# A graph layer on one core: 17 instead of 16 superblocks looked up by a one-hot product, predicated copies in PSUM, and another layout of the turned rows

## What is computed

```python
def reference(x, src, dst, edge_attr_64, edge_weight1, W_node, W_review):
    h = jnp.maximum(_layernorm(x, axis=-1), 0.0)      # 12500 x 16
    m = (h @ W_node.T)[src] + edge_attr_64 @ W_review.T   # 400000 edges
    m = m * edge_weight1
    return x + jax.ops.segment_sum(m, dst, num_segments=12500)
```

## Time and profile before

| what | value |
|---|---|
| median of 3 runs | 1766.9 us (1765.85 to 1771.57) |
| profiled execution, its own time | 1771.62 us |
| its span | 1769.5 us |
| mean granted TensorE clock | 0.942 of full |
| TensorE matmul busy | 1544.8 us (87%), 25,040 instructions |
| VectorE busy | 1455.6 us (82%), 3,393 |
| GpSimd busy | 1247.3 us (70%), 1,177 |
| ScalarE busy | 970.8 us (55%), 4,245 |
| DMA | 195.34 MB, mean 110 GB/s |
| chain that ended last | PE 46%, DVE 24%, issue 12%, DVEq 8%, POOL 6% |

### The profile page before, as it was taken

The page is one execution under the profiler, slowest core; times in us unless marked ns, Lnnn a source line. Parts: engine busy times, 40 slices in busy tenths (PEclk is TensorE's granted clock), DMA queues, the critical chain, the costliest instruction groups (busy, mean ns, idle before and its releaser), DMA issues.

```text
span 1769.5 us, 75737 instructions
## 1 busy us (share of the span) xinstructions
PE 1544.8 (87%) x25040; PEld 1524.7 (86%) x25040; DVE 1455.6 (82%) x3393; ACT 970.8 (55%) x4245; POOL 1247.3 (70%) x1177
## 2 busy tenths in 40 slices
PE   0119998999989899999989998998989998999977
PEld 0019998999989899999989898998989898999975
DVE  7998887888888787888888787878878887878864
ACT  1114364665656564756656564756656564756653
POOL 2287777777777777777777777777777777777400
PEclk9659999999999999999999999999999999999965
DMA  3524345454545445454444454454545454554443
GB/s 116 92 36 113 100 114 114 110 122 103 125 106 128 112 114 127 104 129 109 118 113 111 116 120 116 118 125 105 118 110 114 115 125 109 122 130 100 119 86 48
DMA packets 513913, 195.34 MB, mean 110 GB/s; under 512 B 475071, under 2 KB 496196, under 8 KB 513212
## 3 DMA queue, kind: packets, MB, share of 16 engines
q1 hardware_dynamic: 474853, 178.88, 39.9%
q0 software_dynamic: 36000, 9.29, 5.9%
q10 hardware_dynamic: 2609, 1.55, 0.5%
HBM read 186.67 MB, written 2.92 MB: 107 GB/s over the span
## 4 chain that ended last, share of the span: by engine, by line
PE 46%; DVE 24%; issue 12%; DVEq 8%; POOL 6%; ACT 2%; DMA 1%; ACTq 0%; POOLq 0%; SPq 0%
PE found L1110 26%; PE seg L1143 11%; POOL vals_p L530 6%; DVE big L770 5%; PE seg L1134 5%; DVEq L875 4%; PE edge_h L1124 3%; DVE masked L824 3%; DVEq L867 2%; DVE perm L860 2%; DVE masked L838 1%; DVE mid L845 1%; ACT mid L592 1%; DVE by_rank L715 1%; DVE by_rank L714 1%
## 5 line engine op out<-in xcount | busy, mean ns | idle before, releaser
L530 POOL DMA_INDIRECT vals_p<-h_ext,idx_t x1125 | 1228.7, 1092 | 350.9 <-issue 330.6
L1110 PE MATMUL found<-table,big 128*128 128x112 f16 (+2 forms) x16384 | 870.6, 215 | 57.8 <-DVE by_rank L888 32.3
L1110 PEld LDWEIGHTS found<-table,big 128*128 128x128 f16 x16384 | 846.1, 100 | 63.9 <-DVE by_rank L888 34.9
L592 ACT ACTIVATE sel_p<-hit_p,wgt_t 128x64 f32<-128x64 f16 x1125 | 292.8, 335 | 429.2 <-DVE hit_p L845 416.2
L592 ACT ACTIVATE mid<-mid,wgt_t 128x64 f32<-128x64 f16 x2000 | 500.1, 333 | 36.8 <-DVE mid L845 34.9
L1143 PE MATMUL seg<-mid 128*96 128x64 f32 x4000 | 400.4, 256 | 15.9 <-ACT mid L612 11.3
L1143 PEld LDWEIGHTS seg<-mid 128*96 128x96 f32 x4000 | 379.3, 173 | 18.0 <-ACT mid L592 11.8
L770 DVE TENSOR_SCALAR big<-low_all,own 128x2004 f16<-128x2004 f16 x516 | 361.2, 742 | 2.8 <-DMA low_all<-low_dram 2.8
L879 DVE SCALAR_TENSOR_TENSOR acc<-seg,count_s,acc 96x64 f32 x400 | 112.2, 280 | 168.5 <-issue 126.8
L1134 PE MATMUL seg<-sel_p,vals_p 128*80 128x64 f32 x2250 | 201.8, 237 | 6.9 <-DMA vals_p<-h_ext,idx_t 6.9
L1134 PEld LDWEIGHTS seg<-sel_p,vals_p 128*80 128x80 f32 x2250 | 183.3, 154 | 7.8 <-DMA vals_p<-h_ext,idx_t 3.8
(11 more groups left out here) (131 smaller groups left out, 546.1 us busy)
## 6 DMA issues: line engine op xcount, KB each, us to landing
low_all<-low_dram SPq DMA_DIRECT2D x128, 501.0 KB
mid<-in_edge_attr_dram SPq DMA_DIRECT2D x400, 160.0 KB
vals_p<-in_edge_attr_dram SPq DMA_DIRECT2D x232, 160.0 KB
vals_p<-h_ext,idx_t POOLq DMA_INDIRECT x1125
big<-in_dst_dram SPq DMA_DIRECT2D x1, 1562.5 KB
big<-in_edge_weight_dram SPq DMA_DIRECT2D x1, 1562.5 KB
h_ext<-mid SPq DMA_DIRECT2D x2, 781.2 KB
low_all<-low_dram ACTq DMA_DIRECT2D x2, 501.0 KB
```

The costliest lines, as they stand in the source:

```text
L530: pool.indirect_dma_start(vals_p[:, q % RP, j, R:F], None, h_ext, bass.IndirectOffsetOnAxis(ap=idx_t[:, q * J + j:q * J + j + 1], axis=0), ...
L592: last = nc.scalar.activation(sel[:, j, :], hit[:, j, :], ACT.Copy, scale=wgt_t[:, bass.ds(tile + j, 1)])
L1110: last = nc.tensor.matmul(found[x % 2][:, r * P:r * P + n], hot[:, x // 2 % 2, a, col:col + P], rows, start=(a == 0 and part == 0), stop=( ...
```

## The change

One superblock moves from the gathered edges to the sorted ones: 8 and 17 in place of 9 and 16. That is 200 gathered groups (1,000 indirect DMAs in place of 1,125) and 425 sorted ones, and the loop runs over 16 phases in place of 15. A loop phase has 12 gathered groups, at steps 4 to 15, in place of 14; the first phase has 8, at steps 8 to 15, in place of 15. There are 6 slots for them in place of 7.

The choice among the candidates is made inside `found`, without masks for each candidate: `mark` takes the three bits of the digit and a `valid` flag; where bit 2 is set candidates 4 and up are copied over 0 and up, where bit 1 is set 2 and 3 over 0 and 1, where bit 0 is set 1 over 0; the row that is left is multiplied by `valid` into `found_h`. `masked` is gone, and TensorE waits for `chosen` of the step two before. The four operations are spread over VectorE's step in another way than the four before.

`by_rank` is ordered list, half, feature, so that the 32 values of a list lie next to each other; the casts and the split read PSUM and write `by_rank` in this order.

```diff
-GATHERED = 9
-SORTED = 16
+GATHERED = 8
+SORTED = 17
-RP = 7
-FIRST = 2
+RP = 6
+FIRST = 4
+FIRST0 = 8
 PER_STEPS = STEPS - FIRST
+PER_FIRST = STEPS - FIRST0
...
-        by_rank = by_rank_raw[:, 0:LISTS * H].bitcast(F16).rearrange("p (i f l) -> p i f l", i=2, f=H)
+        by_rank = by_rank_raw[:, 0:LISTS * H].bitcast(F16).rearrange("p (l i f) -> p l i f", i=2, f=H)
...
         def turned_ranks(i):
-            return turn_bank[i].rearrange("p (f l) -> p f l", l=P)[:, :, 0:C]
+            return turn_bank[i].rearrange("p (f l) -> p l f", l=P)[:, 0:C, :]
...
-                        nc.scalar.copy(by_rank[:, 0, i * PART_F:(i + 1) * PART_F, :], turned_ranks(i)).then_inc(rank_top, 1)
+                        nc.scalar.copy(by_rank[:, :, 0, i * PART_F:(i + 1) * PART_F], turned_ranks(i)).then_inc(rank_top, 1)
...
                 def mark(u):
-                    nc.vector.tensor_tensor(mask[:], digit_now[:, bass.ds(u, 1), :].rearrange("p o j -> p (o j)").unsqueeze(1).to_broadcast([C, WIDEST, P]),
-                                            digit[0:C, :].unsqueeze(2).to_broadcast([C, WIDEST, P]), ALU.is_equal).then_inc(mask_in, 1)
+                    nc.vector.tensor_tensor(bits[:], digit_now[:, bass.ds(u, 1), :].rearrange("p o j -> p (o j)").unsqueeze(1).to_broadcast([C, BITS, P]),
+                                            bit_no[:].unsqueeze(2).to_broadcast([C, BITS, P]), ALU.bitwise_and).then_inc(bits_in, 1)
+                    nc.vector.tensor_tensor(valid[:], digit_now[:, bass.ds(u, 1), :].rearrange("p o j -> p (o j)"), limit[:], ALU.is_lt).then_inc(bits_in, 1)
...
-                    nc.vector.tensor_tensor(masked[:], rows_of(x, 0, FOLD), masks_of(x, 0, FOLD), ALU.mult).then_inc(masked_low, 1)
-                    nc.vector.copy_predicated(masked[:, :, 0:WIDTH[x] - FOLD, :], masks_of(x, FOLD, WIDTH[x]), rows_of(x, FOLD, WIDTH[x])).then_inc(masked_in, 1)
-                    nc.vector.tensor_tensor(masked[:, :, 0:2, :], masked[:, :, 0:2, :], masked[:, :, 2:4, :], ALU.add).then_inc(folded, 1)
-                    nc.vector.tensor_tensor(found_h[:, x * RANKS:(x + 1) * RANKS, :], masked[:, :, 0, :], masked[:, :, 1, :], ALU.add).then_inc(chosen, 1)
+                    if WIDTH[x] > HALF:
+                        nc.vector.copy_predicated(rows_of(x, 0, WIDTH[x] - HALF), bit_of(x, 2, WIDTH[x] - HALF), rows_of(x, HALF, WIDTH[x])).then_inc(upper_in, 1)
+                    nc.vector.copy_predicated(rows_of(x, 0, 2), bit_of(x, 1, 2), rows_of(x, 2, 4)).then_inc(pair_in, 1)
+                    nc.vector.copy_predicated(rows_of(x, 0, 1), bit_of(x, 0, 1), rows_of(x, 1, 2)).then_inc(one_in, 1)
+                    nc.vector.tensor_tensor(found_h[:, x * RANKS:(x + 1) * RANKS, :], rows_of(x, 0, 1).rearrange("p j b f -> p j (b f)"),
+                                            valid[:, x * RANKS:(x + 1) * RANKS].unsqueeze(2).to_broadcast([C, RANKS, H]), ALU.mult).then_inc(chosen, 1)
...
                     for step in range(STEPS):
                         if step:
-                            mask_low(u, step - 1)
-                            copy_high(u, step - 1)
+                            copy_upper(u, step - 1)
                         make_hot(u, step)
                         if step:
-                            fold_four(u, step - 1)
+                            copy_pair(u, step - 1)
                         if step:
                             add_of_p(step - 1)
-                            fold_two(u, step - 1)
+                            copy_one(u, step - 1)
                         if step + 1 < STEPS:
                             for g in groups_unsorted(step + 1):
                                 make_perm(t, g)
                         if step:
+                            keep_valid(u, step - 1)
                             add_of_s(step - 1, 0)
...
                     if x >= 2:
-                        if WIDTH[x - 2] == FOLD:
-                            pe.wait_ge(masked_low, ps * (SORTED * STEPS) + u * STEPS + (x - 1))
-                        else:
-                            pe.wait_ge(masked_in, ps * (SORTED * COPIES[STEPS]) + u * COPIES[STEPS] + COPIES[x - 1])
+                        pe.wait_ge(chosen, ps * (SORTED * STEPS) + u * STEPS + (x - 1))
...
-                                                by_rank[:, :, :, g * J + q].rearrange("p i f -> p (i f)"), start=True, stop=True)
+                                                by_rank[:, g * J + q].rearrange("p i f -> p (i f)"), start=True, stop=True)
```

More of the change, by code:

```diff
@@ L39 @@
 WIDEST = 8
-COPIES = [sum(w > WIDEST // 2 for w in WIDTH[:x]) for x in range(STEPS + 1)]
-FOLD = WIDEST // 2
+BITS = 3
+HALF = WIDEST // 2
+UPPERS = [sum(w > HALF for w in WIDTH[:x]) for x in range(STEPS + 1)]
 SHIFT = 2 * NA
@@ L74, with slot_no, first_in @@
 PER_PHASE = PER_STEPS + GROUPS
+PER_FIRST = STEPS - FIRST0
 assert PER_STEPS % RP == 0
 def slot_of(x):
-    return (x - FIRST + 1) % RP
+    return (x - FIRST) % RP
+def slot_no(q):
+    return slot_of(FIRST0 + q)
+def first_in(slot):
+    return [q for q in range(RP) if slot_no(q) == slot][0]
 def step_of(g):
@@ L160, in bass_gnn_preln @@
         ident = sb("ident", [P, P])
-        mask = sb("mask", [C, WIDEST, P], U8)
+        bits = sb("bits", [C, BITS, P], U8)
+        valid = sb("valid", [C, P], U8)
         low_all = sb("low_all", [P, 2, HOT], F16)
         big = sb("big", [P, 2 * NA * HOT // 2 + P * H])
-        masked = sb("masked", [C, RANKS, FOLD, H])
         hot = big[:, 0:NA * HOT].bitcast(F16).rearrange("p (k a n) -> p k a n", k=2, a=NA)
@@ L447, in _ @@
                         low_ahead(0, step, 1)
-                    if step >= FIRST - 1:
-                        sums_p(step - 1, step)
+                    if step >= FIRST0:
+                        sums_p(step - FIRST0, step)
                 with sp.Fori(0, SORTED - 1) as t:
@@ L455, in _ @@
                         if step >= FIRST:
-                            sums_p(t * PER_STEPS + (STEPS - FIRST + 1 + step - FIRST), step)
+                            sums_p(t * PER_STEPS + (PER_FIRST + step - FIRST), step)
                         for g in SUMS[step]:
@@ L502, in _ @@
                 nc.gpsimd.memset(back_row[:, x * RANKS:(x + 1) * RANKS], float(BACK[x]))
+            for k in range(BITS):
+                nc.gpsimd.memset(bit_no[:, k:k + 1], 1 << k)
             nc.gpsimd.memset(turn[:], 0.0)
@@ L1155, in _ @@
                     look_up(0, step)
-                    if step - 2 >= FIRST - 1:
-                        pe.wait_ge(acc_step, ps * NG + (1 + step - 2))
-                    if step >= FIRST - 1:
-                        sum_p(step - 1, (step - 1) // RP, step)
+                    if step - 2 >= FIRST0:
+                        pe.wait_ge(acc_step, ps * NG + (1 + step - 1 - FIRST0))
+                    if step >= FIRST0:
+                        q = step - FIRST0
+                        sum_p(q, (q - first_in(slot_of(step))) // RP, step)
                 turn_ranks(0)
                 with pe.Fori(0, SORTED - 1) as t:
-                    added_t = pe.snap(ps * NG + t * PER_PHASE + (PER_STEPS + 2))
+                    added_t = pe.snap(ps * NG + t * PER_PHASE + (PER_FIRST + 1))
                     for step in range(STEPS):
@@ L1170, in _ @@
                         if step >= FIRST:
-                            q = STEPS - FIRST + 1 + step - FIRST
-                            sum_p(t * PER_STEPS + q, t * (PER_STEPS // RP) + q // RP, step)
+                            q = PER_FIRST + step - FIRST
+                            sum_p(t * PER_STEPS + q, t * (PER_STEPS // RP) + (q - first_in(slot_of(step))) // RP, step)
                         for g in SUMS[step]:
@@ L1179, in _ @@
                         unsort(SORTED - 1, g)
-                    bank_free(ps * NG + (PER_STEPS + 2 + (SORTED - 1) * PER_PHASE), step, True)
+                    bank_free(ps * NG + (PER_FIRST + 1 + (SORTED - 1) * PER_PHASE), step, True)
                     for g in SUMS[step]:
```

128 lines of the change are left out of this document (60 added, 68 removed).

## The result

The changed kernel takes **1791.6 us** (1790.6 to 1792.3) against 1769.2 us (1765.9 to 1771.6) for the one before: a ratio of 1.0125, interval 1.0107 to 1.0143. It is 22 us slower. The forecast was 1797 us and +30. The profiled execution took 1791.1 us, its span is 1789.4.

A forecast was written before the change was run, and what follows sets the result against it. TensorE leads within a phase, VectorE at the turn, GpSimd nearly full. Phases of 94.6 us give +33.5, setup +5.5, phase 0 -7.5, last phase -1: +30.5, scaled to 1797 us; 8-in-10 range 1757 to 1825.

The forecast's parts named there:

- One more superblock costs a whole phase: Phase loop: sixteen phases of 94.6 us instead of fifteen add 33.5 us; phases give back 4 us x 15, which is less.
- break-even of 92.7: Loop phase: the length in us, (1480.1 + 3.0) / 16, at which the change would neither gain nor lose.
- Unsort: TensorE's 125 unsort matmuls a phase: 59.5 ns each falls to 27 with the new layout, 4.1 us per phase.
- the rival at array speed: TensorE's 125 unsort matmuls at 15.8 ns each, with the split free: phase 92.2, 1759 us; chance 0.22.
- Split and cast out of PSUM with a stride: Start of a phase, VectorE's split and ScalarE's casts: strided PSUM reads taken to cost 1.2 us more a phase.
- stays at 0.61 each: Sign against the forecast: VectorE's split operations no dearer, where the four were to take over 2.43 us.
- the split costs in full: Rival, VectorE's split from PSUM: 2.8 us more each phase, phase 96.2, 1823 us; chance 0.15.
- The turn: Start of a phase, up to TensorE's third look_up: net +0.05 from the new wait and +1.2 from the split.
- The new wait: TensorE's look_up waits for `chosen` of two steps before: hidden except at the turn, net +0.05 us a phase.
- would lead if both got more than 1% faster: GpSimd's 70 gathers a phase, 97.0 us: nearly full, the next bound once TensorE and VectorE speed up.
- VectorE's choice: VectorE's step: net -0.6 us, 6.08 becomes 5.5, copies into PSUM no dearer; VectorE follows TensorE with slack.
- Faster: 0.25 (the second case ...): Chance that the changed kernel is faster, made of "the second case and the rest's share"; the rest had 0.05.

## Why the prediction was right, and where not

- **One more superblock costs a whole phase.** Right, and it carries the result: the move costs 81.5 us on the kernel before and 54 us on the one with choice and layout. The measured phase of 93.73 lies 1.0 over the prediction's break-even of 92.7.
- **Unsort.** 27 ns taken, 25 measured; 4.1 us a phase forecast, 34.5 ns x 125 = 4.3 measured, and confirmed by putting the old layout back (3.95 us a phase). The Trainium skill's floor of about 25 ns ("TensorE: Matmul & The Clock Gate", "Wait — 56ns, not 53.3ns?") agrees with this row; the rival at array speed, 15.8 ns, falls.
- **Split and cast out of PSUM with a stride.** 1.2 us a phase was taken and nothing was measured: 672 and 589 ns against 671 and 590. This is the term of the sum that was mis-sized. It was bounded from a strided write in f32, and a strided read is another thing. With 0 the prediction's phase is 93.4. A split that "stays at 0.61 each" is one of the prediction's own signs that its forecast is wrong, and it came. The rival *the split costs in full*, and with it the Trainium skill's rule on PSUM lines applied to these engines ("SBUF — State Buffer", the paragraph on cachelines), falls; of matmuls, of which the rule speaks, nothing here reads PSUM.
- **The turn.** The third look_up was forecast 14.3 us after the turning (13.1 + 1.2); it is 15.2 on the mean, 14.7 and 15.6 in neighbouring phases. Neither the split nor VectorE does it, but TensorE's stall at the loop's jump, 2.7 us on the mean in place of 1.1 and after five matmuls in place of 52, and the lower clock behind both idle times: 0.50 of 2.4 GHz over 867.72 to 871.00, 0.69 over the next lookup, where the turn of the earlier trace rows has 1.00. Neither growth was in the forecast. The stall's comes with the move (the move alone has it). The clock isn't new, only more frequent: over the first lookups of a turn it lies below full in 7 of the 14 turns of the loop before (0.56 to 0.72) and in all 15 after (0.50 to 0.73). The prediction read the turn from a quick one and carried the others as 0.3 us a phase; mean against mean the turn grew by 1.6 us (13.6 to 15.2).
- **The new wait.** "TensorE idle over 1 us ahead of the third look_up, put down to VectorE" is not seen in the loop's turns: TensorE arrives late. That is the second of the prediction's own signs of being wrong that came. It is seen once, at the entry to the loop, where there is no jump behind (216.92, 2.31 us idle), and in each kernel in which TensorE is early: 2.26, 2.34 and 2.33 us. The price of +0.05 was too small; the terms that the prediction lists for it make +0.16 as they stand. `chosen` of step 0 ends 14.2 us after the turning (874.33 + 0.28 - 860.40) where 13.1 was forecast, as VectorE has a stall of 1.77 us of its own at the jump; and a TensorE without its stall is ready for it some 2.3 us before.
- **The rest of a phase.** 78.7 us from the third look_up to the turning, where the forecast's terms make 85.0 - 1.5 - 3.6 = 79.9. Of the 1.2 us more, 0.1 is unsort; the rest isn't put down to one row; short waits within the phase of before (gathers, sums' operands) may be what is gone.
- **GpSimd.** Out of the bound, with 162 us of waiting in 14 phases (11.6 a phase, about 10 forecast). That GpSimd "would lead if both got more than 1% faster" was right in kind, and the layout alone proves it, by 98.0 us of gathers a phase. "Within a phase TensorE leads" fits the kernel before, where GpSimd had 2.4 us a phase to spare. What the prediction lacked is that the price of a gather moves with the order of the other engines' work. The full phase of 97.0 us was the mean over all gathers; in the inner phases 70 make 95.9 to 98.0, as the gather's price moves from 1.069 to 1.099.
- **VectorE's choice.** No dearer into PSUM, and VectorE 7.7 us less busy a phase; the forecast's 0.6 a step were 9.6 with the waits that go. With the move and the old layout its worth on the path is nil (7 us dearer); with the layout in place and no move it is 30 us, by way of GpSimd's gathers. VectorE waits for found rows 52 times in 272 steps, 19.8 us, and not in each as forecast.
- **Chances.** "Faster: 0.25 (the second case ...)" names the wrong case: the faster one is the third of its list, array speed, with 0.22.
- **Outside the loop.** Setup +6.1 (5.5), phase 0 -6.6 (-7.5), last part +0.9 (-1): small, and nearly cancelling.

The forecast of +30.5 us came out at +20. The loop gave +19.6 in place of +33.5, 0.87 a phase, in rounded terms: the turn +0.9 (the split -1.2, stall and clock +2.1), the rest of the phase -1.2, the allowance for disturbance -0.3, and the first phase of the loop, 90.9 us without a jump ahead of it, -0.2 on the mean. The ends gave back 3.4 less than forecast. So the direction came from the right mechanism, while the size came out nearly right in part by luck: the free split and the shorter rest stood against a longer stall and a lower clock that weren't foreseen.

## What to carry over

When two engines are within a few per cent of each other, price a change by what the second one has to spare, not by the first one's gain. Its waits alone understate that (here 13.5 us of 31 in 13 phases), as it also gets ahead. And ask whether its own price stays: here it rose by 26 ns a gather and took nearly all. Moving work off an engine is worth only the gap to the next bound, 96.3 to 93.7 us a phase here, and if the work comes back as one more turn of the loop, the price is a whole turn. A moving operand with a far stride made these short matmuls slow (59.5 ns against 25), and the cure cost nothing where the reader of PSUM did the turning.

## What the runs showed of the hardware

- Engines stall at a loop's jump, each by itself: TensorE 0.5 to 2.6 us in the kernels with 16 superblocks and 2.4 to 3.5 in those with 17; in one turn of the changed kernel TensorE 2.68, VectorE 1.77 and ScalarE 2.65. Two phases in a body take it away inside the body; with all loops so, TensorE's at the jump grew to 3.0 to 4.3.
- After such a stall of 2.68 us TensorE's work ran at the lower of its two clocks (granted 0.50, then 0.69 over the next lookup): 59 matmuls of 64 columns in 3.14 us, 53 ns each. After one of 1.45 us in the earlier trace rows the clock stayed at 1.00.
- ScalarE and VectorE read PSUM with a stride of 512 bytes at the price of a row: 589 and 672 ns for 500 elements.
- In the runs on two other chips TensorE got single instructions 0.73 us apart, and the kernel before took 2702 and 2772 us instead of 1769.
- A gather takes 0.94 us of GpSimd's time by itself and up to 1.88 where it begins just before two of VectorE's `make_perm`. Its mean moves by 26 to 49 ns with the order of the other engines' work, which is 1.8 to 3.4 us a phase when GpSimd is full.
